# Quantised weights passed to a Trainium2 kernel as 8-bit instead of 32-bit integers (state block and gated FFN, eight cores)

## The reference

```python
def _layernorm(x, axis=-1, eps=1e-5):
    m = jnp.mean(x, axis=axis, keepdims=True)
    v = jnp.var(x, axis=axis, keepdims=True)
    return (x - m) / jnp.sqrt(v + eps)

def _qlinear(x, wq, scale):                      # wq: int32 values 0..255
    W = (wq.astype(jnp.float32) - 128.0) * scale[:, None]
    return jnp.einsum('bsd,hd->bsh', x, W)

# x: (16, 2048, 2048) float32; B: (1024, 2048), C: (2048, 1024), D: (2048,)
h = _layernorm(x)
x = x + jnp.einsum('bsn,dn->bsd', jnp.tanh(jnp.einsum('bsd,nd->bsn', h, B)), C) + D * h
h = _layernorm(x)
gate = jax.nn.silu(_qlinear(h, wq_gate, s_gate))  # wq_gate, wq_up: (5632, 2048)
up = _qlinear(h, wq_up, s_up)
x = x + _qlinear(gate * up, wq_down, s_down)      # wq_down: (2048, 5632)
```

## Time and profile before

| | us |
|---|---|
| median of 2 runs | 5401.74 (5397.87 to 5405.61) |
| the profiled execution | 5397.91 |
| its span, core 4, the slowest of eight | 5396.4 |
| spans of the eight cores | 5367.0 to 5396.4 |
| end of the preparation on core 4 (DVE, ACT and SP go on) | 741.7 |

### The profile page before, as it was taken

One profiled execution on the slowest core, in us unless ns is written; L12 is line 12 of the kernel. 1 busy time (PEld: TensorE's weight loads), 2 busy tenths in 40 slices (PEclk: granted clock), 3 DMA queues, 4 the chain that ended last, 5 costly groups with the idle time before them and its releaser, 6 DMA issues.

```text
span 5396.4 us, 51791 instructions; the slowest of 8 cores (5367.0 to 5396.4 us)
## 1 busy us (share of the span) xinstructions
PE 4227.7 (78%) x20368; PEld 2044.2 (38%) x20736; DVE 939.6 (17%) x1408; ACT 397.3 (7%) x576; POOL 93.6 (2%) x179
## 2 busy tenths in 40 slices
PE   0000028999799979998899979996999889988998
PEld 0000014444444444444344444444444444444444
DVE  2222441120211121121112111112112111211100
ACT  0000001000110011100110011001000010001100
POOL 0111100000000000000000000000000000000000
PEclk9999999999899989999999989998999999999999
DMA  9999985455544555455445544555445544563444
GB/s 304 325 327 326 320 268 159 153 180 171 159 153 162 169 157 167 152 176 180 152 152 175 184 145 153 170 160 179 149 153 177 174 150 153 180 195 109 153 148 160
DMA packets 364905, 995.48 MB, mean 184 GB/s; under 512 B 159360, under 2 KB 159360, under 8 KB 337024
## 3 DMA queue, kind: packets, MB, share of 16 engines
q1 hardware_dynamic: 197136, 797.62, 45.4%
q10 hardware_dynamic: 142336, 100.68, 7.2%
q0 software_dynamic: 25200, 93.86, 4.5%
HBM read 847.34 MB, written 111.15 MB: 178 GB/s over the span
## 4 chain that ended last, share of the span: by engine, by line
PE 70%; DMA 22%; DVE 3%; ACT 2%; issue 1%; ACTq 1%; SPq 1%; another core or an unknown queue 0%; DVEq 0%; POOLq 0%
PE PS L601 23%; PE PS L535 21%; PE PS L545 21%; DMA LQ<-wui 4%; DMA LQ<-wdi 4%; DMA LQ<-wgi 4%; PE PS L525 2%; DMA WBB<-sb_img 2%; PE PS L503 2%; DMA WDB<-sd_img 2%; DMA HFM<-HTM 1%; ACT HTM L333 1%; DMA WGU<-su_img 1%; DMA XT<-xin 1%; DMA WCB<-sc_img 1%
## 5 line engine op out<-in xcount | busy, mean ns | idle before, releaser
L535 PE MATMUL PS<-HFM,WGU 128*128 128x512 bf16 (+1 forms) x5784 | 1295.1, 376 | 126.5 <-DMA HFM<-HTM 120.6
L545 PE MATMUL PS<-HFM,WGU 128*128 128x512 bf16 x5512 | 1272.4, 381 | 32.4 <-DMA WGU<-su_img 26.1
L601 PE MATMUL PS<-WDB,GFM 128*128 128x512 bf16 x5520 | 1225.9, 382 | 53.4 <-DMA WDB<-sd_img 47.5
L503 PE MATMUL PS<-HFM,WBB 128*128 128x256 bf16 x2048 | 278.2, 303 | 903.6 <-DMA HFM<-HTM 821.7
L535 PEld LDWEIGHTS PS<-HFM,WGU 128*128 128x128 bf16 x5888 | 588.5, 100 | 781.4 <-issue 127.2
L601 PEld LDWEIGHTS PS<-WDB,GFM 128*128 128x128 bf16 x5632 | 554.4, 98 | 724.8 <-issue 70.5
L545 PEld LDWEIGHTS PS<-HFM,WGU 128*128 128x128 bf16 x5632 | 552.9, 98 | 698.0 <-issue 42.5
L472 DVE SCALAR_TENSOR_TENSOR GFM<-PS,SUC,GFM 128x512 bf16<-128x512 f32 x352 | 264.2, 751 | 2236.2 <-PE PS L545 2236.2
L503 PEld LDWEIGHTS PS<-HFM,WBB 128*128 128x128 bf16 x2048 | 218.0, 108 | 963.8 <-issue 916.5
L350 ACT ACTIVATE GFM<-PS,SGC 128x512 bf16<-128x512 f32 x352 | 241.3, 687 | 2155.6 <-PE PS L535 2155.4
L525 PE MATMUL PS<-WCB,SFM 128*128 128x512 bf16 x992 | 249.0, 390 | 29.9 <-DMA WCB<-sc_img 28.2
(11 more groups left out here) (29 smaller groups left out, 347.7 us busy)
## 6 DMA issues: line engine op xcount, KB each, us to landing
WGU<-sg_img SPq DMA_DIRECT2D x352, 512.0 KB, 3.3
WGU<-su_img SPq DMA_DIRECT2D x352, 512.0 KB, 3.3
WDB<-sd_img SPq DMA_DIRECT2D x321, 512.0 KB, 3.4
WBB<-sb_img SPq DMA_DIRECT2D x128, 512.0 KB, 5.7
LQ<-wgi SPq DMA_DIRECT2D x44, 1024.0 KB, 47.2
LQ<-wui SPq DMA_DIRECT2D x44, 1024.0 KB, 46.7
LQ<-wdi SPq DMA_DIRECT2D x44, 1024.0 KB, 36.5
XT<-xin ACTq DMA_DIRECT2D x32, 1024.0 KB, 9.0
```

Source lines behind the costliest of these rows:

```text
L503: ins = tensor.matmul(PS[:, n, lo:hi], WBB[u % 3][:, c, :], HFM1[:, c, lo:hi], start=(c == 0), stop=(c == DC - 1))
L535: ins = tensor.matmul(PS[:, 4 + hc % 2, lo:hi], WGU[t % 3][:, c, :], HFM2[:, c, lo:hi], start=(c == 0), stop=(c == DC - 1))
L545: ins = tensor.matmul(PS[:, 6 + hc % 2, lo:hi], WGU[t % 3][:, c, :], HFM2[:, c, lo:hi], start=(c == 0), stop=(c == DC - 1))
L601: ins = tensor.matmul(PS[:, bank, :], GFM[:, hc, g * 128:(g + 1) * 128], WDB[u % 3][:, q * 512:(q + 1) * 512], start=(hc == 0), stop=(hc = ...
```

## The change

The three integer inputs are declared as unsigned 8-bit, the `LQ` buffers too, and the host converts the arrays (their values, 0 to 255, fit). A load of a G, U or D unit then moves 2048 bytes in each partition in place of 8192. The operations, their number and order, all waits, the buffers' number, the bfloat16 images and the main stage stay as they are: on every engine each instruction stands where it stood before, with the same waits.

```diff
+U8 = mybir.dt.uint8
...
-    wgi = nc.dram_tensor("wgi", [HC, 128, DC * 128], I32, kind="ExternalInput").ap()
-    wui = nc.dram_tensor("wui", [HC, 128, DC * 128], I32, kind="ExternalInput").ap()
-    wdi = nc.dram_tensor("wdi", [SL * 11, 128, D], I32, kind="ExternalInput").ap()
+    wgi = nc.dram_tensor("wgi", [HC, 128, DC * 128], U8, kind="ExternalInput").ap()
+    wui = nc.dram_tensor("wui", [HC, 128, DC * 128], U8, kind="ExternalInput").ap()
+    wdi = nc.dram_tensor("wdi", [SL * 11, 128, D], U8, kind="ExternalInput").ap()
...
-            LQ = [P_(nc.sbuf_tensor(f"LQ{i}", [128, D], I32)) for i in range(10)]
+            LQ = [P_(nc.sbuf_tensor(f"LQ{i}", [128, D], U8)) for i in range(10)]
...
-    wg = np.ascontiguousarray(np.asarray(L0_ffn_wq_gate, dtype=np.int32))
+    wg = np.ascontiguousarray(np.asarray(L0_ffn_wq_gate, dtype=np.int32).astype(np.uint8))
```

More of the change, by code:

```diff
@@ L621 @@
     Dv = np.asarray(L0_attn_D, dtype=np.float32)
-    wg = np.ascontiguousarray(np.asarray(L0_ffn_wq_gate, dtype=np.int32))
-    wu = np.ascontiguousarray(np.asarray(L0_ffn_wq_up, dtype=np.int32))
-    wd = np.ascontiguousarray(np.asarray(L0_ffn_wq_down, dtype=np.int32))
+    wg = np.ascontiguousarray(np.asarray(L0_ffn_wq_gate, dtype=np.int32).astype(np.uint8))
+    wu = np.ascontiguousarray(np.asarray(L0_ffn_wq_up, dtype=np.int32).astype(np.uint8))
+    wd = np.ascontiguousarray(np.asarray(L0_ffn_wq_down, dtype=np.int32).astype(np.uint8))
     sg = np.asarray(L0_ffn_s_gate, dtype=np.float32)
```

## The result

| | us |
|---|---|
| median of all 11 runs of the changed kernel | 5149.36 (5071.52 to 5811.91) |
| median of all 10 runs of the kernel before | 5405.44 (5389.35 to 5785.57) |
| ratio to before | 0.9448, 95% interval 0.9407 to 0.9489 |
| the profiled execution, changed kernel | 5116.6 |
| its span, core 5, the slowest | 5115.1 |

In some of the runs of both kernels the cores of one die had a lower clock; the two medians contain these runs, so that the 5149 lies above the forecast's range, and the ratio leaves them out. On the 5401.74 us that the forecast started from, the ratio makes 5104 us (5081 to 5126), 298 us less. The forecast was 5079 us, with a range of 5050 to 5132. Faster by over 2% has come, and the time lies in the range, in its slower half.

What follows compares the result with a forecast made beforehand. The preparation was taken as bound by DMA bytes, the main stage by TensorE. 84.5 + 202.4 + 130.7 + 3.9 = 421.5 us against 741.8, with 4655 unchanged, gave 5077.6, forecast as 5079 us, range 5050 to 5132.

Steps and rivals of the forecast that it cites:

- The step in G and U: Time per unit in the preparation's 88 G and U units: 2.3 us, midway between 2.18 and 2.40, 202.4 us in all.
- the plain way: A G or U unit's 0.786 MB over the unchanged 327 GB/s: 2.40 us a unit.
- DVE at 1227 ns, POOL and the buffers: In G and U: conversions stay at 1227 ns, POOL issues stores fast enough, eight WOUT buffers suffice (12.9 of 18.4 us).
- The start: Preparation before G and U: first G unit at 84.5 us instead of 88.66, a gain of 4.2 us.
- D: The preparation's last 44 units: 105.6 us at 2.4 each, plus 21.6 and 3.5 for slices and SDP, 130.7 us.
- The slice starts: DVE's waits at slice beginnings in D: three of 7.2 us, 21.6 us, plus 3.5 us at the first slice.
- The end and the main stage: Preparation's last store unchanged at 3.9 us; the main stage after it keeps its 4655 us.
- Small packets: Rival: 2 KB load packets cost nearly as much as 4 KB in G, U, D; 70 us more, 5149; chance 0.12.
- Starved stores: Rival: POOL writes store descriptors only between DVE conversions; G and U step 2.75 us, 40 us more, 5119; chance 0.08.
- One element a cycle for 8 bits: Rival: DVE converts 8-bit sources at one element a cycle; G and U step 2.4 us, total 5088; chance 0.06.
- The memory slower for stores: Rival: memory takes stores at half rate; step 4 us or more, preparation gain under 108 us; chance 0.03.
- Slower than before: Rival: DVE needs several cycles per 8-bit element; at 9.17 us an operation the kernel takes some 5980 us; chance 0.01.

## Why the prediction was right, and where it was off

*What bounds the kernel* was right: two stages, the first bound by the bytes of loads and stores, and only that one moved.

*The step in G and U* was the term that was mis-sized: 2.3 us predicted, 2.40 to 2.47 measured on the eight cores (2.45 on the profiled one, 214 us for 202.4, 12 us). The failed step is the price of a packet: 0.161 us for a store of 4 KB, and a quarter of 0.444 us for a load of 2 KB, which gave 2.18 us and pulled the forecast down from the 2.40 of the plain way. Both prices were the queue's share of full engines in that one mix. In the changed kernel the same store packet shows 68.4% of 16 x 214 us over some 10800 data packets, 0.217 us, at nearly the same total rate.

What a packet costs can be worked out from the steps instead (an estimate). Stores alone take 1.51 us for 8 packets on an engine, 0.189 us each. What the other steps leave for their 8 load packets is 0.118 us each for 2 KB (2.45 us), 0.218 for 4 KB (3.25, uint16) and 0.416 for 8 KB (4.84, before). Two runs test that: the doubled loads should take 1.51 + 16 x 0.118 = 3.39 us and took 3.37; the loads in pairs should take 1.51 + 4 x 0.218 = 2.38 and took 2.34 to 2.42. So the direction of "stores are cheaper for a byte than loads" was right, 0.189 against 0.218 us at 4 KB, but the prediction had 0.161 against half of 0.444. Of the 0.27 us between 2.18 and 2.45, 0.22 are the store packets' and 0.05 the load packets'. As rates, the mixes give 325 GB/s before (1.573 MB in 4.84 us), 323 with uint16, 320 with 8 bits, 334 with pairs and 350 for stores alone: near each other, but not the same. The plain way, bytes over the rate of the stretch, gave 2.40, the low end of what was measured, and would have been nearer.

The argument that "half the 8 KB packet and the 4 KB packet agree within a tenth" does not come out either: 0.222 and 0.197 us are an eighth apart, and the 0.197 is from the main stage, where the DMA share is 0.5.

*DVE at 1227 ns, POOL and the buffers* held. That the stores queue was allowed for ("if stores queue instead of loads, the DMA engines are still what is full"), and four and twelve buffers show it. The step does not follow DVE's operation either: at 694 ns it was longer.

*The start* came at 86.05 instead of 84.5 us on the profiled core, 1.5 us late: DVE's wait in front of the first G unit shrank from 4.25 to 1.34 us and not to 0.1.

*D* was right in its sum by two errors that cancel. Predicted 130.7 us; measured from 300.47 to the end of the last conversion, 429.9 + 2.3 = 432.2, 131.7 us. DVE needs 2.20 us from start to start, not 2.4, since operations overlap a little when the next is ready (24.31 us for eleven, each recorded at 2.28): 44 x 2.2 = 97, 9 us less. The slice starts cost 34.5 us instead of 25.1. In the 9.3 us gap 2.43 MB moved, not the 1.96 that I listed, as more of the following loads and stores slips in. A line through the earlier trace rows and this gap (an estimate, and from two points only) has some 1.8 us of fixed time and 3.1 us for each MB; I had scaled without a fixed part.

*The end and the main stage.* The last store took 4.1 us for 3.9. The main stage took 4678.7 us on the slowest core for the 4655 assumed, 24 us, the largest single miss. Stages as long are in runs of other kernels, the one before among them (above), so the miss is spread between executions and not the change's. The granted clock accounts for it only in part. The 0.963 of that core and the 0.967 in the earlier trace rows can't be set side by side, since the preparation, at a clock of 1.00, is a smaller part of the shorter span. With it taken out (an estimate) the main stages had some 0.9595 and 0.9615, worth 10 of the 24 us. Where the rest of the spread comes from was not tried.

The sum for the profiled execution: 12 (G and U) + 1.5 + 1 + 0.2 + 24 = 39 us over the 5077.6 worked out, which is 5116.6.

*The rivals.* Small packets: a real price, 4% of a step where all loads are of 2 KB and doubled, and worth 10 us when the loads come in pairs (in both runs the number of loads changed with it), where the rival asked for 70. Starved stores: the mechanism is there, the cost is not. One element a cycle for 8 bits: fallen, by the 1227 ns. The memory slower for stores: fallen, stores alone reach 350 GB/s. Slower than before: fallen.

The range held with its own terms off: the preparation's gain was 14 us smaller than forecast, the main stage's spread could have gone the other way, and D came out right by two errors that cancelled, which is luck.

What stays open is whether the some 320 GB/s are the limit of the core's DMA engines (their share reads 1.00 to 1.05) or of the memory with eight cores at work. No run had idle cores beside it.

## What to carry to other kernels

For a stretch with a DMA share of 1, divide the new bytes by the rate that the stretch itself shows; a queue's time for each packet moves when the mix does and is no price. A price comes from a run in which only one kind moves, and it needs a second run to test it. When the bytes fall, look where the engine that was covered comes out (here DVE in D) and where single buffers make the whole queue restart; spreading bytes over another full stretch gives little, dropping them gives their full time. The row that says which buffer an engine waits for tells where the queue stands: change the buffers' number before you believe that it sets the pace.

## What was not expected of the hardware

- VectorE takes uint8 to bfloat16 in 1227 ns for 128 x 2048, exactly as int32, but uint16 in 694 ns.
- GpSimd's issue of a DMA is held until 0.11 to 0.12 us after the end of a VectorE conversion of one source that runs at the time (58 of 62 issues with stores alone); two were recorded with 1.06 and 1.20 us instead of 0.53. A conversion of two sources did not hold it. Moving the stores to ScalarE's queue changed no step, because the DMA engines were full (share 1.03 and 1.04).
- The time of a 4 KB store packet went from 0.161 to 0.217 us when the loads beside it shrank to a quarter, at nearly the same total rate (327 and 319 GB/s); stores alone make it 0.189 us.
- Two-source conversions in a row start 2.20 us apart though each is recorded at 2.28.
